# Routing weights of a fused two-layer kernel: ScalarE spreads them, the split is made after the transpose, and the scale products use four row groups

## The chip, the cores and the metric

The kernel runs on one core of one Trainium2 chip. The metric is the device time of one execution in microseconds; the time before is the median of three runs.

## What is computed

Input x has 2048 tokens (32 batches of 64) of 1024 features, float32. Two layers follow each other, each adding its result to x. Only the first one is touched by the change. Its core, cut to what matters:

```
y          = agg_w[b] @ x[b] + agg_b[b]           # 64x64 mix per batch
logits     = y @ gate_w.T                         # 1024 -> 8 experts
routing    = softmax(logits)                      # per token, 8 weights
in_scale   = routing @ in_channel_scale           # 8 -> 1024
out_scale  = routing @ out_channel_scale          # 8 -> 1024
x1         = x + (y * in_scale) @ sign(W).T * out_scale + bias
```

The second layer is a grouped convolution along the features, followed by a 1024x1024 product and a low-rank term with eight experts.

## The kernel before

The tokens are cut into 16 tiles of 128, taken in pairs (i, p). The program has a stage for each layer; the first runs over all tiles and writes x1 to a scratch tensor in DRAM, the second reads it back. Every engine has its own program, written out by hand in a fixed order with semaphores between them; loops run over the pairs, and nothing is reordered by a planner.

In the first stage TensorE works on two tiles at once. The large product of tile t (ffn0_step, L429) has 32 steps of 128x512: two output halves of 16, each half with the rounded part of the input (a = 0) and the rest (a = 1), so that float32 precision is kept with the faster float32r type. Between these steps stand the small products of tile t+1: ahead of step 0 the mixing product y (product_y, L382), ahead of step 12 (LOGITS_AT) the logits (product_logits, L391), ahead of step 20 (TURN_AT) the transpose of the routing weights (turn_routing, L397), ahead of step 24 (SCALES_AT) the products that make the two scales (product_in_scale, L405, and product_out_scale, L411).

Between the logits and the transpose stands a chain over two engines. VectorE takes the maximum (L756), ScalarE the exponentials and their sum (L601), VectorE the reciprocal (L758), the normalised weights (L762), a float32r copy of them (L766) and the rest that the rounding left (L768). The copies lie in the tile routing as 64 used columns: for the input scale two times [hi, hi, lo, lo] of 8 experts, for the output scale the same; 64 more columns are zero. After the transpose ScalarE copies 64 rows to routing_t (L605). The scales' weights scale_w hold hi and lo rows in the alternating order, so that one product over 32 rows gives all four terms of hi/lo. The input scale uses rows 0 to 31 for eight products of 128x128, the output scale rows 32 to 63 for two of 128x512. VectorE then multiplies y by the input scale (scale_in, L775), ScalarE rounds the product (round_parts, L610), and VectorE takes the rest (take_rest, L782). For the tile before, VectorE multiplies with the output scale (scale_out, L790), which ScalarE has copied out of PSUM (L621).

GpSimd does three kinds of SBUF work beside this: x plus bias (add_bias0, L895), the sum x1 (make_x1, L903), and the rests of the second layer's weights (rest_of_stage, L907), one chunk for every pair. SyncE issues the DMAs.

The first tile is special: nothing overlaps it, so y of both first tiles is made before the logits of the first (L435 to L438). The y of the second goes to banks 6 and 7, which the output scale would use, and the output scale of the first tile is therefore made later (L461 to L464), once VectorE has read these banks.

## Time and profile before

| | us |
|---|---|
| runs | 618.63, 617.22, 616.88 |
| median | 617.22 |
| profiled execution, first to last instruction | 617.4 |
| TensorE busy in it | 591.4 (96%) |
| VectorE busy | 252.3 (41%) |
| ScalarE busy | 113.5 (18%) |
| GpSimd busy | 147.0 (24%) |

The first stage lasts to about 249 us, the second takes the rest. TensorE's row says how long matmuls were under way, not that the array ran at its peak: matmuls are pipelined and weight loads are recorded apart (PEld). The chain of work that ended last is 89% TensorE, 4% VectorE and 1% ScalarE; the VectorE part is nearly all at the lines of the routing weights.

### The profile page before, as it was taken

Reading aid. Unit: us, or ns where it says so; the run is one execution under the profiler, and the core shown is the slowest. Engines: PE = TensorE matmul, PEld = TensorE weight load, DVE = VectorE, ACT = ScalarE, POOL = GpSimd, SP = SyncE. Lnnn points to the kernel's source line nnn. Section 1 sums busy time; section 2 is a strip of 40 time slices with the busy share of each in tenths; the row PEclk is TensorE's granted clock in tenths of the full one; section 3 lists DMA queues with packets and bytes.
Section 4 is the critical chain, followed back from the end, with each engine's and each line's share of the span. In section 5 each row is a group of like instructions: output and inputs, shape, how many; then the busy total and the mean of one; then the engine's idle time right before and its main releaser. Section 6 shows DMA issues by size and latency. Waiting matters only on the chain.

```text
span 617.4 us, 9165 instructions
## 1 busy us (share of the span) xinstructions
PE 591.4 (96%) x3381; PEld 516.5 (84%) x3381; DVE 252.3 (41%) x479; ACT 113.5 (18%) x255; POOL 147.0 (24%) x79
## 2 busy tenths in 40 slices
PE   4799999999999999999999999999999999999997
PEld 3677878778787878988988988988988998998996
DVE  4547766666775655623123123123123123123122
ACT  4522222222222213301101101101101101101100
POOL 0324345453444344801101101101101101101100
PEclk9769999999997999999999999999999999999999
DMA  9903242332323348512311312311321321321100
GB/s 291 355 1 112 89 140 102 108 110 72 110 84 98 112 131 188 141 63 45 107 70 37 106 71 35 106 72 34 106 74 32 106 75 31 106 78 28 69 35 34
DMA packets 36110, 58.15 MB, mean 94 GB/s; under 512 B 4096, under 2 KB 24384, under 8 KB 36096
## 3 DMA queue, kind: packets, MB, share of 16 engines
q1 hardware_dynamic: 35952, 57.70, 30.0%
q10 hardware_dynamic: 144, 0.26, 0.1%
q8 instruction: 10, 0.16, 0.1%
q14 instruction: 4, 0.03, 0.0%
HBM read 41.15 MB, written 16.79 MB: 94 GB/s over the span
## 4 chain that ended last, share of the span: by engine, by line
PE 89%; DVE 4%; ACT 1%; issue 0%; DVEq 0%
PE bank L498 47%; PE bank L429 17%; PE bank L480 9%; PE bank L391 4%; PE bank L382 4%; PE bank L526 4%; DVE gate L762 3%; PE bank L405 2%; PE bank L411 1%; PE bank L397 1%; ACT gate L601 1%; DVE routing L768 0%; DVE routing L766 0%; DVE gate L756 0%; DVE gate L758 0%
## 5 line engine op out<-in xcount | busy, mean ns | idle before, releaser
L498 PE MATMUL bank<-early,parts 128*128 128x320 f32 (+1 forms) x1152 | 206.5, 337 | 0.0
L498 PEld LDWEIGHTS bank<-early,parts 128*128 128x128 f32 x1152 | 184.7, 188 | 15.7
L429 PE MATMUL bank<-late,parts 128*128 128x512 f32 x512 | 140.6, 420 | 0.7 <-ACT parts L610 0.7
L429 PEld LDWEIGHTS bank<-late,parts 128*128 128x128 f32 x512 | 97.3, 200 | 22.9 <-issue 4.2
L935 POOL TENSOR_TENSOR work<-work,bias_bc 128x1024 f32<-128x1024 f32 x16 | 38.7, 2422 | 285.8 <-DMA work<-x_scratch 285.8
L498 PE MATMUL bank<-late,parts 128*128 128x512 f32 x384 | 93.9, 393 | 0.0
L498 PEld LDWEIGHTS bank<-late,parts 128*128 128x128 f32 x384 | 70.9, 188 | 15.8
L903 POOL TENSOR_TENSOR work<-work 128x512 f32<-128x512 f32 x32 | 40.8, 1276 | 80.4 <-DVE work L790 80.4
L480 PE MATMUL bank<-band,raw 128*128 128x128 f32 x512 | 59.7, 275 | 0.0
L480 PEld LDWEIGHTS bank<-band,raw 128*128 128x128 f32 x512 | 59.0, 192 | 0.1
L610 ACT ACTIVATE parts<-work 128x512 fp32r<-128x512 f32 x64 | 40.0, 633 | 74.8 <-DVE work L827 43.7
L782 DVE TENSOR_TENSOR parts<-work,parts 128x512 fp32r<-128x512 f32 x64 | 45.9, 739 | 12.0 <-ACT parts L610 10.5
L895 POOL TENSOR_TENSOR work<-xs,bias_bc 128x1024 f32<-128x1024 f32 x16 | 38.5, 2406 | 47.1 <-ACT late L594 24.6
L849 DVE TENSOR_TENSOR qk<-bank,qk 128x256 f32<-128x256 f32 x16 | 6.8, 424 | 100.5 <-ACT qk L666 100.5
L868 DVE TENSOR_TENSOR wh_t<-bank,wh_t 128x128 fp32r<-128x128 f32 x16 | 4.7, 292 | 95.0 <-ACT wh_t L674 95.0
L878 DVE TENSOR_TENSOR work<-bank,work 128x512 f32<-128x512 f32 x32 | 22.1, 692 | 50.4 <-PE bank L526 50.4
L382 PEld LDWEIGHTS bank<-agg,xs 128*128 128x128 f32 x256 | 34.6, 212 | 1.4 <-issue 0.2
L382 PE MATMUL bank<-agg,xs 128*128 128x128 f32 x256 | 34.8, 296 | 0.0
L391 PEld LDWEIGHTS bank<-cst,work 128*128 128x128 f32 x256 | 32.7, 200 | 1.3
L391 PE MATMUL bank<-cst,work 128*128 128x8 f32 x256 | 31.1, 257 | 0.0
L775 DVE TENSOR_TENSOR work<-bank,work 128x512 f32<-128x512 f32 x32 | 20.8, 687 | 23.7 <-PE bank L405 23.6
L526 PE MATMUL bank<-lora,wh_t 128*128 128x512 f32 x96 | 27.6, 396 | 0.0
(90 smaller groups left out, 363.5 us busy)
## 6 DMA issues: line engine op xcount, KB each, us to landing
xs<-in_x SPq DMA_DIRECT2D x16, 512.0 KB, 3.7
x_scratch<-work SPq DMA_DIRECT2D x16, 512.0 KB, 2.9
raw<-x_scratch SPq DMA_DIRECT2D x128, 64.0 KB, 3.1
work<-x_scratch SPq DMA_DIRECT2D x16, 512.0 KB, 3.6
out_tokens<-work SPq DMA_DIRECT2D x15, 512.0 KB, 2.7
stage<-in_wearly SPq DMA_DIRECT2D x8, 576.0 KB, 3.8
row_bc<-token_rows_scratch SPq DMA_DIRECT2D x30, 64.0 KB, 3.6
work<-in_wsign SPq DMA_DIRECT2D x3, 512.0 KB, 12.6
```

The costliest lines, as they stand in the source:

```text
L382: last = mm(bank[b0 + h][:, c * P:(c + 1) * P], xs[:, p, at:at + P], agg[:, p, :], start=True, stop=True)
L391: last = mm(bank[2][:, 0:E], y_t[:, c, :], cst[:, C_GATE + c * E:C_GATE + (c + 1) * E], start=(c == 0), stop=(c == L8 - 1))
L429: last = mm(bank[4 + h][:, :], parts[:, p, a, c, :], signs[:, c, h * HALF:(h + 1) * HALF], start=(k % 16 == 0), stop=(k % 16 == 15))
L480: last = mm(bank[n // 4][:, (n % 4) * P:(n % 4 + 1) * P], raw[:, p, n, s:s + P], band[:, s * GROUPS + n % 4, :], start=(s == 0), stop=(s = ...
L498: return mm(dst, parts[:, p, a, c, :], w(b, c), start=(k == 0), stop=(close and k == 23))
L526: last = mm(o[h][:, :], wh_t[:, a, :], lora[:, b, h * HALF:(h + 1) * HALF], start=False, stop=(k == 2))
L610: do(cols(parts[:, p, 0], h), cols(y_t, h), ACT.Copy).then_inc(done, 1)
L782: v.tensor_tensor(cols(parts[:, p, 1], h), cols(y_t, h), cols(parts[:, p, 0], h).bitcast(F32), ALU.subtract).then_inc(done, 1)
L878: v.tensor_tensor(o, bank[4 + 2 * p + h][:, :], o, ALU.add).then_inc(out_ready, 1)
L895: g.tensor_tensor(resid[:, p, :], xs[:, p, :], bias_bc[:, :], ALU.add).then_inc(xb_ready, 2)
L903: g.tensor_tensor(resid[:, p, cols], os_sb[:, cols], resid[:, p, cols], ALU.add).then_inc(x1_ready, 1)
L935: g.tensor_tensor(resid[:, p, :], resid[:, p, :], bias_bc[:, :], ALU.add).then_inc(resid_ready, 1)
```

## The change

The normalised weights are no longer made by VectorE. After the reciprocal, ScalarE multiplies the eight exponentials by it and writes them sixteen times side by side, as 128 plain float32 columns (spread_routing). After the transpose all 128 rows are in PSUM. ScalarE rounds them into routing_hi (round_routing), and VectorE makes routing_t in one instruction, (row factor times routing_hi) plus the PSUM rows (split_routing). The factor, a column of the constants, is 0 for the rows that should stay and minus 1 for those that should hold the rest.

The rows of scale_w now are four groups of 32: input scale left half, input scale right half, output scale left half, output scale right half. It is 128x512 instead of 64x1024. product_scales does the ten products in an order that goes round the groups. SCALES_AT goes from 24 to 26. On VectorE split_routing stands ahead of scale_out of the tile before. In the first tile, y of the second tile comes after the logits of the first and goes to banks 0 and 1, and the output scale is made with the input scale, so the separate later step is gone.

```diff
-LOGITS_AT, TURN_AT, SCALES_AT, CONV0_AT = 12, 20, 24, 8
+LOGITS_AT, TURN_AT, SCALES_AT, CONV0_AT = 12, 20, 26, 8
...
-            sp.dma_start(bias_bc[0:64, :], scales).then_inc(scales_loaded, 16)
+            sp.dma_start(bias_bc[:, 0:HALF], scales).then_inc(scales_loaded, 16)
...
-            def product_in_scale(i, p):
-                pe.wait_ge(routing_copied, 2 * i + p + 1)
-                for h in range(2):
-                    for c in range(4):
-                        at = (4 * h + c) * P
-                        last = mm(bank[2 + h][:, c * P:(c + 1) * P], scale_w[0:32, at:at + P], routing_t[0:32, :],
-                                  start=True, stop=True)
-                    last.then_inc(in_scale_done, 1)
-
-            def product_out_scale():
-                for h in range(2):
-                    mm(bank[6 + h][:, :], routing_t[32:64, :], scale_w[32:64, h * HALF:(h + 1) * HALF],
-                       start=True, stop=True).then_inc(out_scale_done, 1)
+            def product_scales(i, p):
+
+                pe.wait_ge(routing_split, 2 * i + p + 1)
+                for c in range(4):
+                    for h in range(2):
+                        rows = slice(32 * h, 32 * h + 32)
+                        made = mm(bank[2 + h][:, c * P:(c + 1) * P], scale_w[rows, c * P:(c + 1) * P],
+                                  routing_t[rows, :], start=True, stop=True)
+                        if c == 3:
+                            made.then_inc(in_scale_done, 1)
+                    if c < 2:
+                        rows = slice(64 + 32 * c, 96 + 32 * c)
+                        mm(bank[6 + c][:, :], routing_t[rows, :], scale_w[rows, :], start=True,
+                           stop=True).then_inc(out_scale_done, 1)
...
             product_y(0, 0)
-
-            product_y(0, 1, 6)
             product_logits(0, 0)
+            product_y(0, 1)
             pe.wait_ge(scale_ready, 1)
-            pe.wait_ge(routing_zeroed, 1)
             turn_routing(0, 0)
-            product_in_scale(0, 0)
+            product_scales(0, 0)
...
-                    if k == LOGITS_AT - 4 and first_tile:
-
-                        pe.wait_ge(y_biased, 4)
-                        product_out_scale()
...
-            def copy_routing(i, p):
+            def spread_routing(i, p):
+
+                act.wait_ge(gate_rcp, 2 * i + p + 1)
+                do(routing[:, :].rearrange("p (a e) -> p a e", e=E),
+                   gate[:, 8:16].rearrange("p (a e) -> p a e", a=1).broadcast_to([P, P // E, E]), ACT.Copy,
+                   scale=gate[:, 4:5]).then_inc(routing_ready, 1)
+
+            def round_routing(i, p):
                 act.wait_ge(routing_turned, 2 * i + p + 1)
-                do(routing_t[:, :], bank[3][0:64, 0:P], ACT.Copy).then_inc(routing_copied, 1)
+                do(routing_hi[:, :], bank[3][:, 0:P], ACT.Copy).then_inc(routing_rounded, 1)
...
                 v.reciprocal(gate[:, 4:5], gate[:, 1:2]).then_inc(gate_rcp, 1)
-                dve.wait_ge(gate_rcp, t1)
-
-                dve.wait_ge(routing_ready, t1 - 1)
-                v.tensor_scalar(gate[:, 32:40], gate[:, 8:16], gate[:, 4:5], None, ALU.mult).then_inc(gate_prob, 1)
-                dve.wait_ge(gate_prob, t1)
-
-                prob = gate[:, 32:40].rearrange("p (a b e) -> p a b e", a=1, b=1).broadcast_to([P, 2, 2, E])
-                v.tensor_copy(routing[:, 0:2, 0:2, :], prob).then_inc(routing_hi, 1)
-                dve.wait_ge(routing_hi, t1)
-                v.tensor_tensor(routing[:, 0:2, 2:4, :], prob, routing[:, 0:2, 0:2, :].bitcast(F32),
-                                ALU.subtract).then_inc(routing_ready, 1)
+
+            def split_routing(i, p):
+
+                dve.wait_ge(routing_rounded, 2 * i + p + 1)
+                v.scalar_tensor_tensor(routing_t[:, :], routing_hi[:, :].bitcast(F32), cst[:, C_RLO:C_RLO + 1],
+                                       bank[3][:, 0:P], ALU.mult, ALU.add).then_inc(routing_split, 1)
```

VectorE, one period of the first stage, before: L756 to L768 make the routing weights of the next tile, L790 is scale_out of this one, L775 and L782 are scale_in and take_rest.

```order
L756 TENSOR_REDUCE gate<-bank 128x1
L758 RECIPROCAL gate<-gate 128x1
L762 TENSOR_SCALAR gate<-gate 128x8
L766 CAST routing<-gate 128x2x16
L768 TENSOR_TENSOR routing<-gate,routing 128x2x16
L790 TENSOR_TENSOR work<-bank,work 128x512
L775 TENSOR_TENSOR work<-bank,work 128x512 x2
L782 TENSOR_TENSOR parts<-work,parts 128x512 x2
L790 TENSOR_TENSOR work<-bank,work 128x512
```

The same period after the change (the line numbers are those of the changed kernel: L755 is the maximum, L784 scale_out).

```order
L755 TENSOR_REDUCE gate<-bank 128x1
L757 RECIPROCAL gate<-gate 128x1
L762 SCALAR_TENSOR_TENSOR routing_t<-routing_hi,cst,bank 128x128
L784 TENSOR_TENSOR work<-bank,work 128x512
L769 TENSOR_TENSOR work<-bank,work 128x512 x2
L776 TENSOR_TENSOR parts<-work,parts 128x512 x2
L784 TENSOR_TENSOR work<-bank,work 128x512
```

Three small instructions before the transpose are gone, and one that waits for the transpose stands ahead of scale_out.

TensorE, one period, from the transpose (L397) to the end of the 32 steps (L429); L405 makes the input scale and L411 the output scale.

```order
 L397 MATMUL bank<-cst,routing 128x128
-L429 MATMUL bank<-late,parts 128x512 x4
-L405 MATMUL bank<-routing_t,scale_w 128x128 x8
-L411 MATMUL bank<-scale_w,routing_t 128x512 x2
-L429 MATMUL bank<-late,parts 128x512 x8
+L429 MATMUL bank<-late,parts 128x512 x6
+L405 MATMUL bank<-routing_t,scale_w 128x128 x2
+L411 MATMUL bank<-scale_w,routing_t 128x512
+L405 MATMUL bank<-routing_t,scale_w 128x128 x2
+L411 MATMUL bank<-scale_w,routing_t 128x512
+L405 MATMUL bank<-routing_t,scale_w 128x128 x4
+L429 MATMUL bank<-late,parts 128x512 x6
```

The ten products are the same in number and size; they stand two steps later and in mixed order.

TensorE in the first tile, up to the place where the scale products begin (L382 is y, L391 the logits).

```order
-L382 MATMUL bank<-agg,xs 128x128 x16
+L382 MATMUL bank<-agg,xs 128x128 x8
 L391 MATMUL bank<-cst,work 128x8 x8
+L382 MATMUL bank<-agg,xs 128x128 x8
 L397 MATMUL bank<-cst,routing 128x128
-L405 MATMUL bank<-routing_t,scale_w 128x128 x8
-L429 MATMUL bank<-late,parts 128x512 x8
-L411 MATMUL bank<-scale_w,routing_t 128x512 x2
-L429 MATMUL bank<-late,parts 128x512 x4
```

Eight products of y have moved behind the logits, and the output scale no longer stands between step 7 and step 8.

## Rows read from the trace of the kernel before

**Rows 1.** The page: the span, and TensorE's granted clock in forty slices

```profile
span 617.4 us, 9165 instructions
...
PEclk9769999999997999999999999999999999999999
```

**Rows 2.** Waits, all: engine, line, waited for, us in total, times, longest

```profile
PE bank L397 <- DVE routing L768: 11.3, 8, 1.6
```

**Rows 3.** Timeline, tile with a wait: start us, us, engine, line, operation [idle before]

```profile
106.35 0.17 DVE L756 TENSOR_REDUCE gate<-bank 128x1 f32<-128x8 f32 x1 [1.70 <-PE bank L391]
...
106.74 2.38 POOL L895 TENSOR_TENSOR work<-xs,bias_bc 128x1024 f32<-128x1024 f32 x1
...
107.14 2.00 DVE L762 TENSOR_SCALAR gate<-gate 128x8 f32<-128x8 f32 x1
...
109.64 0.33 PE L397 MATMUL bank<-cst,routing 128*128 128x128 f32 x1 [1.36 <-DVE routing L768]
```

**Rows 4.** Timeline, the tile before that one, which has no wait

```profile
92.76 2.37 POOL L895 TENSOR_TENSOR work<-xs,bias_bc 128x1024 f32<-128x1024 f32 x1 [3.17 <-DMA x_scratch<-work]
...
94.63 0.53 DVE L762 TENSOR_SCALAR gate<-gate 128x8 f32<-128x8 f32 x1
```

**Rows 5.** Two lines of stage two: duration ns min/median/max, first and last start

```profile
L862 DVE SCALAR_TENSOR_TENSOR wh<-gate,bank x16: 348/348/349, 259.5 to 604.1; 128x128 f32<-128x128 f32 x16
...
L674 ACT ACTIVATE wh_t<-bank x16: 277/278/279, 265.0 to 607.4; 128x128 fp32r<-128x128 f32 x16
```

**Rows 6.** Chain in order of time, around the scale products: start us, us, what

```profile
96.91 0.70 PE bank L405 x5
...
98.08 2.04 PE bank L429 x8
```

**Rows 7.** Timeline of weight loads and one matmul in the same scale products

```profile
96.84 0.63 PEld L405 LDWEIGHTS bank<-routing_t,scale_w 32*128 32x128 f32 x5 [0.36 <-issue]
...
97.35 0.18 PEld L411 LDWEIGHTS bank<-scale_w,routing_t 32*128 32x128 f32 x1
97.35 0.49 PE L411 MATMUL bank<-scale_w,routing_t 32*128 32x512 f32 x1
...
97.51 0.30 PEld L405 LDWEIGHTS bank<-routing_t,scale_w 32*128 32x128 f32 x2
```

**Rows 8.** The input scale's products: duration ns min/median/max

```profile
L405 PE MATMUL bank<-routing_t,scale_w x128: 267/271/468, 24.0 to 235.5; 32*128 32x128 f32 x128
```

**Rows 9.** Stretches: busy us of PE, PEld, DVE, ACT, POOL, then granted clock

```profile
137.00:143.00 6.00, 6.00 (x29) 4.62 (x28) 3.27 (x5) 1.71 (x3) 1.19 (x1) 0.72 0.00 0
193.00:201.00 8.00, 8.00 (x34) 6.81 (x34) 4.46 (x7) 2.35 (x4) 1.36 (x2) 0.57 0.02 8
```

**Rows 10.** Timeline of TensorE in the first tile

```profile
13.39 6.46 PE L382 MATMUL bank<-agg,xs 128*128 128x128 f32 x32
...
23.18 0.45 PE L397 MATMUL bank<-cst,routing 128*128 128x128 f32 x1 [1.65 <-DVE routing L768]
...
26.61 3.78 PE L429 MATMUL bank<-late,parts 128*128 128x512 f32 x8 [0.65 <-ACT parts L610]
32.16 1.22 PE L411 MATMUL bank<-scale_w,routing_t 32*128 32x512 f32 x2 [1.77 <-DVE work L749]
...
35.18 3.42 PE L391 MATMUL bank<-cst,work 128*128 128x8 f32 x16
...
42.00 0.41 PE L397 MATMUL bank<-cst,routing 128*128 128x128 f32 x1
```

**Rows 11.** Timeline of GpSimd and VectorE in the first tile

```profile
25.02 5.15 POOL L895 TENSOR_TENSOR work<-xs,bias_bc 128x1024 f32<-128x1024 f32 x2 [24.57 <-ACT late L594]
25.14 0.69 DVE L775 TENSOR_TENSOR work<-bank,work 128x512 f32<-128x512 f32 x1 [2.10 <-PE bank L405]
...
26.60 4.12 DVE L782 TENSOR_TENSOR parts<-work,parts 128x512 fp32r<-128x512 f32 x2
```

**Rows 12.** Stretch at the half clock in the first tiles, columns as in rows 9

```profile
33.30:42.10 8.80, 8.80 (x31) 7.53 (x30) 2.42 (x8) 2.07 (x5) 3.14 (x2) 0.50 0.01 2
```

More of the change, by code:

```diff
@@ L87, in adaln_ffn_kernel @@
         stage = sb("stage", [P, 2, NW])
-        scale_w = sb("scale_w", [64, H], F32R)
+        scale_w = sb("scale_w", [P, HALF], F32R)
         parts = sb("parts", [P, 2, 2, L8, P], F32R)
@@ L98, in adaln_ffn_kernel @@
         row_bc = sb("row_bc", [P, 2, P])
-        routing = sb("routing", [P, 4, 4, E], F32R)
-        routing_t = sb("routing_t", [64, P], F32R)
+        routing = sb("routing", [P, P])
+        routing_hi = sb("routing_hi", [P, P], F32R)
+        routing_t = sb("routing_t", [P, P], F32R)
         gate = sb("gate", [P, 64])
@@ L381, in product_y @@
                         at = (4 * h + c) * P
-                        last = mm(bank[b0 + h][:, c * P:(c + 1) * P], xs[:, p, at:at + P],
+                        last = mm(bank[h][:, c * P:(c + 1) * P], xs[:, p, at:at + P],
                                   agg[:, p, :], start=True, stop=True)
@@ L396, in turn_routing @@
                 pe.wait_ge(routing_ready, 2 * i + p + 1)
[L397 to L412 removed]
+                nc.tensor.transpose(bank[3][:, 0:P], routing[:, :], ident).then_inc(routing_turned, 1)
+            def product_scales(i, p):
[11 more added lines that the diff above has]
+                           stop=True).then_inc(out_scale_done, 1)
             def ffn0_step(i, p, k, first_tile=False):
@@ L585, in _ @@
             do(row_bc[:, :, :].rearrange("p a n -> p (a n)"), bank[4][:, 0:2 * P], ACT.Copy).then_inc(first_rows_ready, 1)
-            act.wait_ge(rows_loaded, 16)
             act.wait_ge(scales_loaded, 16)
-            do(scale_w[:, :], bias_bc[0:64, :], ACT.Copy, scale=rws[:, R_SG:R_SG + 1]).then_inc(scale_hi, 1)
+            do(scale_w[:, :], bias_bc[:, 0:HALF], ACT.Copy, scale=cst[:, C_SSG:C_SSG + 1]).then_inc(scale_hi, 1)
             def take_signs(c):
@@ L693, in _ @@
             v.memset(agg[:, :, :], 0.0).then_inc(agg_zeroed, 1)
-            v.memset(routing[:, 2:4, :, :].bitcast(F32), 0.0).then_inc(routing_zeroed, 1)
             dve.wait_ge(rows_loaded, 16)
@@ L795, in period0 @@
             def period0(i, p, ni, q, mix_next=True, first=False):
-                add_mix_bias(ni, q, b0=6 if first else 0, first_rows=first)
+                add_mix_bias(ni, q, first_rows=first)
                 if mix_next:
@@ L800, in period0 @@
                 route(ni, q)
+                split_routing(ni, q)
                 scale_out(i, p, 0)
@@ L807, in _ @@
             route(0, 0)
+            split_routing(0, 0)
             scale_in(0, 0)
@@ L970, in lay_out @@
     rows[0:K8, R_BK:R_BK + S] = f["L0_cond_bias_k"]
-    is_lo = (np.arange(64) // E) % 2
-    rows[:, R_LO] = is_lo
-    rows[:, R_SG] = 1 - 2 * is_lo
+    consts[:, C_RLO] = -((np.arange(P) // (2 * E)) % 2)
+    consts[:, C_SLO] = (np.arange(P) // E) % 2
+    consts[:, C_SSG] = 1 - 2 * consts[:, C_SLO]
     batch = np.arange(B)[:, None]
@@ L978, in lay_out @@
     mix = np.tile(f["L0_cond_weight"].reshape(K8, S, S).transpose(2, 1, 0), (2, 1, 1))
-    scales = np.concatenate([np.tile(perm(f["L0_ffn_in_channel_scale"], 1), (4, 1)),
-                             np.tile(perm(f["L0_ffn_out_channel_scale"], 1), (4, 1))])
+    scales = np.concatenate([np.tile(perm(f[name], 1)[:, h * HALF:(h + 1) * HALF], (4, 1))
+                             for name in ("L0_ffn_in_channel_scale", "L0_ffn_out_channel_scale") for h in range(2)])
     wsign = turned(perm(f["L0_ffn_weight"], 0))
```

29 lines of the change are left out of this document (13 added, 16 removed).

## The prediction

> **What bounds the kernel now.** First the page: the profiled execution spans 617.4 us and the median of the runs is 617.22 us, so what lies around the span is nothing that counts (0.2 us less), and the sum below is made against 617.4. TensorE is busy 96% of the span, and its granted clock is full in nearly all of the forty slices, with dips at the start and twice in the first third [rows 1]. So only what TensorE does or waits for counts, and since the change touches the first stage only, the second (from 249 us on) keeps its length.
>
> Then the waits. One is repeated: the transpose of the routing weights (L397) waits for VectorE's last routing instruction, 8 times, 11.3 us in total [rows 2]. The first of them, in the first tile, is 1.65 us [rows 10], so seven in the steady part hold 9.7 us, 1.38 us each.
>
> Then the timeline of one such tile. After the logits, VectorE's maximum starts at 106.35. The normalising instruction L762, on eight columns, takes 2.00 us and ends at 109.14, and GpSimd's L895, from 106.74 for 2.38 us, ends at 109.12 [rows 3]. In the tile before, which has no wait, L762 takes 0.53 us and ends at 95.16, with GpSimd's L895 ending at 95.13 [rows 4]. So the small instruction ends when GpSimd's ends, whatever its own work: it is held by the SBUF work of GpSimd. In every second tile GpSimd is later, because the weight rests (L907) stand in front of L895, and there TensorE has to wait.
>
> **The wait before the transpose.** The change takes L762, L766 and L768 off the path and puts one ScalarE instruction there. Price of the spread, 128 columns: the trace has no such form from SBUF; the nearest row is a 128x128 copy out of PSUM, 0.278 us [rows 5]. I take 0.32, with 0.28 and 0.45 as ends. From the maximum's start to the end of the reciprocal 0.76 us pass (106.35 to just before 107.14 [rows 3]), with 0.05 for the semaphore and 0.32 the weights are ready 1.15 us after it, at 107.5. TensorE came free at 109.64 - 1.36 = 108.28. The wait is gone with 0.8 us in hand, even at the dear end. Term: **-9.7 us**.
>
> Would GpSimd hold something else instead? The new VectorE instruction L762 (split) reads one tensor in SBUF and one in PSUM. A VectorE instruction with the same kinds of operands, L775, started at 25.14 inside GpSimd's 25.02 to 30.17 and took its usual 0.69 us, while L782, with both tensors in SBUF, needed 4.12 us for two [rows 11]. So the split should not be held.
>
> **The wait before the scale products.** The split costs more after the transpose than the old copy did. Transpose 0.33 [rows 3], rounding on ScalarE 0.28, split 0.35 [rows 5], three semaphores of 0.04: 1.08 us. TensorE has six steps there instead of four; eight steps take 2.04 us [rows 6], so six take 1.53. The cover is 0.45 us; if it fails, TensorE pays the difference in each of 15 tiles. Queued behind the split on VectorE is scale_out of the tile before, which began before the transpose and now ends some 1.8 us after it. GpSimd's x1 waits for it, and so does step 0 of the next tile, which comes after the scale products, six steps and y, over 3 us later; scale_in, next on VectorE, has its data no earlier than that. I cost it at nothing. The six steps and y that follow the scale products (1.5 + 1.8 us) must hide scale_in, the rounding and the first rest: 0.69 + 0.63 + 0.69 = 2.0 us. They do.
>
> **The scale products.** Now the ten take 98.08 - 96.91 = 1.17 us [rows 6]. The five weight loads of one row group begin in 0.63 - 0.19 = 0.44 us, 0.11 us apart, and L411, in the other row group, starts in between without moving them: L405's last two still start from 97.51, and L411 itself is 0.49 us under way [rows 7]. So products of different row groups run side by side and those of one group follow at 0.11 us. After the change the longest group has four products instead of eight: 4 x 0.11 = 0.44 us less. The two 512-column products begin third and sixth and are within that time nearly. I take 0.40 us less for each of 15 tiles: **-6.0 us**. Bounds: 0.5 us less each (-7.5), and ten loads in a row at 0.11, that is two steps more than the eight of now, +0.22 (+3.3).
>
> The Trainium skill, TensorEngine Tiling, section Theoretical Speedup, promises up to four times for contractions of 32 rows or less. By that the block would shrink from 1.17 to 0.29 us and the term would be -13 us. The rows above show one overlap of two groups and not four, so the page's figure carries no part of the sum. The same page, section Key Properties, says that changing the tiling mode drains TensorE, which speaks against more switching; between the groups of one size the rows show no drain.
>
> **The clock.** In two stretches, 137 to 143 and 193 to 201 us, the mean granted clock is 0.72 and 0.57 [rows 9]: 3.4 and 6.9 us at the lower level, 1.2 GHz, which cost half of that, 5.1 us. Both follow a tile in which TensorE had been idle before the transpose; in the whole second stage, without such waits, the clock never falls [rows 1]. I expect them gone: **-5.1 us**, with 0 as the other end.
>
> **The first tile.** Two waits stand there: 1.65 us before the transpose, and 1.77 us before the output scale at 32.16 [rows 10]. The first is filled by the second y (half of 6.46 us [rows 10]), which stood ahead of the logits. As the chain from logits to step 0 grows by the split and by a y that has to be finished, step 0 begins only some 0.4 us before 26.61. The second wait goes with the output scale: it waited for VectorE's rests, held by GpSimd (4.12 us for two [rows 11]), and for the bias after them. Now steps 8 to 11 go on at once (four at 0.43 = 1.7 us, where 35.18 - 32.16 = 3.0 us passed) and the logits wait for the bias, which comes at 32.1 - 0.4 - 0.7 = 31.0. The second logits start near 31.4 instead of 35.18: 3.8 us. All this ran at the lower clock, still 0.50 from 33.3 to 42.1 [rows 12]. If the clock rises as long after work becomes continuous as it did there, it does so near 35 instead of 42, ahead of the transpose at 42.00 - 3.8 = 38.2; the 3.2 us between are then done in half. Together 5.4; I take **-5.0 us**, with -3 and -8 as ends. The smaller edits (a shorter scale_w, its load over 128 rows, no zeroing of routing) lie beside TensorE's work.
>
> **Sum.** 617.4 - 9.7 - 6.0 - 5.1 - 5.0 = 591.6 us of span, less 0.2: 591.5.
>
> **Rivals.**
> - The scale products get no cheaper: four groups share something that two did not. The term is then 0 to +3.3 instead of -6: 597.5 to 601. For it: only two groups are seen together. Against it: nothing in the step of 0.11 us moved when the second group came in.
> - The clock still falls twice in the first stage: 596.6. For it: the ten small products use a part of the array only. Against it: no fall without a wait in the second stage.
> - The split is held by GpSimd after all. In every second tile L895 runs over the time of the split, 0.9 us more than the cover: seven times 0.9 is 6.3, so 598. Against it stands L775 [rows 11].
> - Slower than before: each switch of row group waits for the matmul before it. The products would then stand one behind the other at their full durations, eight at 0.27 [rows 8] and two at 0.49 [rows 7], 3.1 us instead of 1.17, in 16 tiles +32 us: 591.5 + 6 + 32 = 629.5. It decides from about 2.4 us for the block, where the other terms are used up (19.8 us over 16 tiles is 1.2 us). Now there is one switch, then nine. Against it: the first switches in the rows cost nothing.
> - The change does not do what it says: the weights come as late as before, because ScalarE is not free when the reciprocal ends: about 617. Against it: its two instructions end before 107 and it waits for the transpose.
>
> **How the numbers follow.** Chances: the forecast 0.63, no cheaper products 0.15, clock 0.12, held split 0.05, switches 0.03, no effect 0.02. The range from 586.5 to 602.0 holds the forecast with its own ends (first tile at -8, products at -7.5) and the first three rivals with little more than 0.05 outside them; the rest of the 0.2 is for two rivals at once. About 0.3% is what a measurement of this kernel can tell from no change. Faster by more than that: 0.95; the same: 0.02; slower: 0.03.
>
> **What would show it.** In the changed kernel the waits list should have no entry of the transpose for a routing instruction beyond the first tile; the transpose should follow the eighth step at once; the distance from the first scale product to the next step should be near 0.8 us; L762 (split) should take 0.35 us in all tiles, also under GpSimd's L895; the tile period should be near 12.3 us throughout; the granted clock should stay at 1.00 from about 35 us on. The forecast is wrong if a wait of the scale products for the split appears, if their block stays at 1.1 us or more, or if the clock's dips remain.

## The result and the profile after

| | before | after |
|---|---|---|
| runs, us | 618.63, 617.22, 616.88, 617.7 | 585.94, 587.87, 587.86, 585.37 |
| median, us | 617.46 | 586.9 |
| ratio (95% interval) | | 0.950 (0.948 to 0.952) |
| span of the profiled execution, us | 617.4 | 584.2 |
| mean granted clock in it | 0.974 | 0.994 |

The forecast was 591.5 with a range from 586.5 to 602.0. Executions of the kernel after fall into two groups 2 us apart (585.4 to 585.9 and 587.9) and those of before spread over some 3 us (616.9 to 618.6 here), the profiled execution of before is one of the longer and that of after one of the shorter, and spans are compared below within a group as far as their times tell it.

The page of the kernel after, which answers [rows 1]: the span, busy time of the engines, and the granted clock in forty slices.

```profile
span 584.2 us, 9131 instructions
...
PE 569.8 (98%) x3381; PEld 502.3 (86%) x3381; DVE 232.6 (40%) x446; ACT 118.9 (20%) x271; POOL 148.1 (25%) x79
...
PEclk9889999999999999999999999999999999999999
```

The dips of the slices in the middle of the first stage are gone. So is the repeated wait of [rows 2]: this is TensorE's part of the list of waits from the first y on (line, waited for, us, times, longest), and no entry has L397 in it.

```profile
PE bank L429 <- ACT parts L609: 1.5, 1, 1.5
PE bank L405 <- DVE routing_t L762: 1.0, 1, 1.0
...
PE bank L391 <- DVE work L748: 0.5, 1, 0.5
```

Each of the three stands once, before the second transpose. Behind that TensorE waits for nothing that the profile shows in the first stage.

The timeline of a tile in which GpSimd's sum (now L891) runs, to set beside [rows 3, 4]. Columns: start us, us, engine, line, operation, idle before and its releaser. L598 is the spread, L604 the rounding, L762 now the split.

```profile
80.13 0.17 DVE L755 TENSOR_REDUCE gate<-bank 128x1 f32<-128x8 f32 x1 [1.16 <-PE bank L391]
80.19 2.41 POOL L891 TENSOR_TENSOR work<-xs,bias_bc 128x1024 f32<-128x1024 f32 x1 [3.20 <-DMA x_scratch<-work]
...
80.92 0.40 ACT L598 ACTIVATE routing<-gate 128x128 f32<-128x128 f32 x1 [0.23 <-DVE gate L757]
...
81.90 0.27 PE L397 MATMUL bank<-cst,routing 128*128 128x128 f32 x1
...
82.52 0.35 DVE L762 SCALAR_TENSOR_TENSOR routing_t<-routing_hi,cst,bank 128x128 fp32r<-128x128 f32 x1 [1.64 <-ACT routing_hi L604]
...
83.49 0.33 PE L405 MATMUL bank<-routing_t,scale_w 32*128 32x128 f32 x2
```

The weights are ready at 81.32, 1.19 us after the maximum began, while GpSimd works until 82.60. TensorE takes them at 81.90, behind its eighth step. The split ends at 82.87, the first scale product starts 0.62 us later.

The two new instructions over all 16 tiles (duration in ns: least, median, most; first and last start), to set beside [rows 5]; the single product of L405 is unchanged, 267 to 325 ns against [rows 8]:

```profile
L598 ACT ACTIVATE routing<-gate x16: 400/402/403, 20.0 to 199.4; 128x128 f32<-128x128 f32 x16
...
L762 DVE SCALAR_TENSOR_TENSOR routing_t<-routing_hi,cst,bank x16: 346/347/348, 21.5 to 201.0; 128x128 fp32r<-128x128 f32 x16
```

The chain of work that ended last, in order of time (start us, us, what), in the same tile, for [rows 6]:

```profile
82.06 0.11 PE bank L397
82.17 1.39 PE bank L429 x6
83.56 0.26 PE bank L405 x2
83.81 0.10 PE bank L411
83.92 0.23 PE bank L405 x5
84.15 1.58 PE bank L429 x6
...
93.90 0.11 PE bank L397
```

The ten scale products hold the chain from 83.56 to 84.15, 0.59 us where it was 1.17. The tile's period is 93.90 - 82.06 = 11.84 us, for 12.3 forecast. A second thing is in the chain and was in no term of the forecast: the transpose's piece is 0.11 us. In the kernel before it was three times as long in 13 of the 14 tiles from the third transpose on (0.31 or 0.33 us), also in six of the seven without a listed wait. Its chain in the tile of [rows 6], with the second transpose and the start of the second stage (L498):

```profile
42.21 0.21 PE bank L397
...
95.67 0.31 PE bank L397
...
248.73 1.31 PE bank L498 x9
```

The same two places in the kernel after (L491 is now the second stage):

```profile
34.52 0.21 PE bank L397
...
215.16 1.90 PE bank L491 x13
```

From the second transpose to the second stage 206.52 us have become 180.64; the second stage, from there to the end of the span, took 368.7 and takes 369.0.

TensorE in the first tile, for [rows 10]:

```profile
21.94 0.33 PE L405 MATMUL bank<-routing_t,scale_w 32*128 32x128 f32 x2 [0.97 <-DVE routing_t L762]
...
24.11 4.62 PE L429 MATMUL bank<-late,parts 128*128 128x512 f32 x12 [1.50 <-ACT parts L609]
29.22 1.92 PE L391 MATMUL bank<-cst,work 128*128 128x8 f32 x16 [0.50 <-DVE work L748]
```

The waits before the transpose (1.65) and before the output scale (1.77) of [rows 10] have gone. In their place stand 0.97 for the split and 0.50 for the bias, and the wait before step 0 has grown from 0.65 to 1.50. VectorE's two rests are still held by GpSimd there, as in [rows 11]:

```profile
24.09 4.21 DVE L776 TENSOR_TENSOR parts<-work,parts 128x512 fp32r<-128x512 f32 x2 [0.16 <-ACT parts L609]
```

The first stretch of [rows 9] in the kernel after, same columns (the second has a clock of 1.00 too; busy us of PE, PEld, DVE, ACT, POOL, then granted clock):

```profile
137.00:143.00 6.00, 6.00 (x42) 4.96 (x40) 2.44 (x6) 2.00 (x5) 4.83 (x2) 1.00 0.72 214
```

### The profile page after: what moved, and what is told of

The parts are those of the page before. It is cut to its first block, busy times and chain, and to the rows that moved or that the text cites. A ratio compares the mean times of both kernels' runs of the same rounds, so it can differ in the third digit from the quotient of the medians.

```text
span 584.2 us, 9131 instructions
## 1 busy us (share of the span) xinstructions
PE 569.8 (98%) x3381; PEld 502.3 (86%) x3381; DVE 232.6 (40%) x446; ACT 118.9 (20%) x271; POOL 148.1 (25%) x79
## 4 chain that ended last, share of the span: by engine, by line
PE 94%; DVE 0%; issue 0%
PE bank L491 49%; PE bank L429 21%; PE bank L473 10%; PE bank L391 4%; PE bank L382 4%; PE bank L519 4%; PE bank L405 1%; PE bank L397 0%; PE bank L512 0%; PE bank L411 0%; DVE work L748 0%; DVE work L874 0%
## 5 line engine op out<-in xcount | busy, mean ns | idle before, releaser
L491 PE MATMUL bank<-early,parts 128*128 128x320 f32 (+1 forms) x1152 | 206.5, 337 | 0.0
L491 PEld LDWEIGHTS bank<-early,parts 128*128 128x128 f32 x1152 | 184.7, 188 | 15.7
L429 PE MATMUL bank<-late,parts 128*128 128x512 f32 x512 | 134.5, 411 | 1.5 <-ACT parts L609 1.5
L429 PEld LDWEIGHTS bank<-late,parts 128*128 128x128 f32 x512 | 93.5, 193 | 21.9 <-ACT parts L609 1.9
L491 PE MATMUL bank<-late,parts 128*128 128x512 f32 x384 | 94.2, 394 | 0.0
L491 PEld LDWEIGHTS bank<-late,parts 128*128 128x128 f32 x384 | 70.9, 188 | 16.1
L891 POOL TENSOR_TENSOR work<-xs,bias_bc 128x1024 f32<-128x1024 f32 x16 | 38.7, 2424 | 45.3 <-DMA x_scratch<-work 23.1
L874 DVE TENSOR_TENSOR work<-bank,work 128x512 f32<-128x512 f32 x32 | 22.1, 692 | 50.7 <-PE bank L519 50.7
L382 PEld LDWEIGHTS bank<-agg,xs 128*128 128x128 f32 x256 | 32.5, 200 | 1.4 <-issue 0.2
L391 PEld LDWEIGHTS bank<-cst,work 128*128 128x128 f32 x256 | 31.4, 194 | 2.0 <-issue 0.9
L382 PE MATMUL bank<-agg,xs 128*128 128x128 f32 x256 | 33.0, 285 | 0.0
L391 PE MATMUL bank<-cst,work 128*128 128x8 f32 x256 | 30.1, 253 | 0.5 <-DVE work L748 0.5
L664 ACT ACTIVATE qk<-bank 128x64 f32<-128x64 f32 x16 | 3.6, 225 | 119.0 <-PE bank L491 119.0
```

Of the source, the lines that this page charges most:

```text
L382: last = mm(bank[h][:, c * P:(c + 1) * P], xs[:, p, at:at + P], agg[:, p, :], start=True, stop=True)
L391: last = mm(bank[2][:, 0:E], y_t[:, c, :], cst[:, C_GATE + c * E:C_GATE + (c + 1) * E], start=(c == 0), stop=(c == L8 - 1))
L429: last = mm(bank[4 + h][:, :], parts[:, p, a, c, :], signs[:, c, h * HALF:(h + 1) * HALF], start=(k % 16 == 0), stop=(k % 16 == 15))
L491: return mm(dst, parts[:, p, a, c, :], w(b, c), start=(k == 0), stop=(close and k == 23))
L874: v.tensor_tensor(o, bank[4 + 2 * p + h][:, :], o, ALU.add).then_inc(out_ready, 1)
L891: g.tensor_tensor(resid[:, p, :], xs[:, p, :], bias_bc[:, :], ALU.add).then_inc(xb_ready, 2)
```

## The experiments

Twelve kernels were run, in three batches (e1 to e4, e5 to e8, e9 to e12), each on another chip. Each batch had its own runs of the kernel before, to which the ratios refer; their medians were 617.47, 616.09 and 617.37 us. The kernel after was not run in them, so against it a difference of less than about 1.5 us can't be told from medians alone. Diffs are against the kernel after, unless said.

**One row group or two instead of four.** Does the gain of the products come from the row groups, or from the mixed order?

e1_two_groups:

```diff
-                        rows = slice(32 * h, 32 * h + 32)
+                        rows = slice(0, 32)
...
-                        rows = slice(64 + 32 * c, 96 + 32 * c)
+                        rows = slice(64, 96)
```

> The changed kernel with the ten scale products in two row groups instead of four: both halves of the input scale from rows 0 to 31, both of the output scale from rows 64 to 95, in the same order. It leaves out that the halves have weights of their own, so its output is not that of the layer; the work is the same in number and size. If products of different row groups run side by side and those of one group follow at 0.11 us, the longest group has eight again: the block goes from 0.59 to 1.0 to 1.17 us, the kernel from 586.9 to 594 to 596. If instead the gain came from the order of the products or from the copies out of PSUM, it stays at 587.

e2_one_group has `slice(0, 32)` in both places.

> The changed kernel with all ten scale products in one row group, rows 0 to 31, in the same order; as in e1 the output scale and the right half of the input scale get the wrong weights. By the theory of side-by-side groups nothing overlaps: eight products at 0.11 and two at 0.22 us, with the start 1.5 to 1.6 us for the block instead of 0.59, times 16: 601 to 603. If the block is bound by issue, it stays under 1 us and the kernel under 593.

Measured: e1 592.1 us, ratio 0.964 (0.956 to 0.971), with one execution of 600.47 among three at 591.9 to 592.3, of which there is no trace and for which nothing was found. e2 601.89 us, ratio 0.974 (0.971 to 0.977). The block of e1 in its chain:

```profile
84.94 0.25 PE bank L405
...
85.53 0.45 PE bank L405 x4
85.98 1.58 PE bank L429 x6
```

and of e2:

```profile
89.83 0.36 PE bank L405 x2
...
91.33 1.59 PE bank L429 x6
```

The end of the block in the kernel before, in the tile of [rows 6]:

```profile
97.61 0.11 PE bank L411
97.73 0.22 PE bank L405 x2
97.95 0.13 PE bank L411
```

The block lasts 1.50 us in one group, 1.04 in two and 0.59 in four. The kernel before, with two groups and the two output products among the last, had 1.17: the order, with another pair of rows in e1, is worth 0.13, the step from two groups to four 0.45. In the span e1 is 590.4 and the kernel after 584.2 (same group), 6.2 us, where 15 times 0.45 is 6.75. e2 is 600.4 against 586.0 in the longer group, 14.4, where 15 times 0.91 is 13.7. e1 came 2 us below what was expected (594 to 596), e2 as expected. The rivals "no cheaper" and "switches cost" fall.

The four groups gain 2.5 times over one. The Trainium skill, TensorEngine Tiling (Array Packing), section Theoretical Speedup, gives up to four times for contractions of 32 rows. An estimate from that figure is 1.50 / 4 = 0.38 us for the block; the measurement, 0.59, decides.

**The order of the first tile.** e3_old_first_tile puts the old order back: the second y ahead of the logits and into banks 6 and 7, the output scale apart.

```diff
             product_y(0, 0)
+            product_y(0, 1, 6)
             product_logits(0, 0)
-            product_y(0, 1)
...
-            product_scales(0, 0)
+            product_scales(0, 0, False)
...
+                    if k == LOGITS_AT - 4 and first_tile:
+                        pe.wait_ge(y_biased, 4)
+                        product_out(0)
+                        product_out(1)
```

> The changed kernel with the first tile's order of before: the second tile's y ahead of the first logits and in banks 6 and 7, the output scale of the first tile ahead of step 8. The second transpose began at 42.0 us before and at 34.3 us after. If the new order brought most of these 7.7 us, it begins near 40 and the kernel takes 592 to 593; if they came from the four row groups, the split and the clock alone, it begins by 36 and the kernel takes under 589.

Measured: 592.96 us, ratio 0.960 (0.958 to 0.963), as expected. Its timeline has the wait for the output scale back, and the second transpose comes when it came in [rows 10]:

```profile
32.09 0.79 PE L401 MATMUL bank<-scale_w,routing_t 32*128 32x512 f32 x2 [1.37 <-DVE work L755]
...
41.52 0.41 PE L397 MATMUL bank<-cst,routing 128*128 128x128 f32 x1
```

The order of the first tile is worth 6 us, and it is separable from the rest. A part of it is TensorE's rate: the second logits take 3.42 us in e3 and 1.92 in the kernel after. Behind that tile e3 has the same periods as the kernel after, with the granted clock at 1.00 from 42 to 220 us.

**Only the hold.** e4_before_psum is the kernel before with one thing changed: the exponentials and their normalised form lie in PSUM.

```diff
-                do(gate[:, 8:16], bank[2][:, 0:E], ACT.Exp, bias=gate[:, 0:1], accum_out=gate[:, 1:2]).then_inc(gate_exp, 1)
+                do(bank[2][:, 16:24], bank[2][:, 0:E], ACT.Exp, bias=gate[:, 0:1], accum_out=gate[:, 1:2]).then_inc(gate_exp, 1)
...
-                v.tensor_scalar(gate[:, 32:40], gate[:, 8:16], gate[:, 4:5], None, ALU.mult).then_inc(gate_prob, 1)
+                v.tensor_scalar(bank[2][:, 32:40], bank[2][:, 16:24], gate[:, 4:5], None, ALU.mult).then_inc(gate_prob, 1)
...
-                prob = gate[:, 32:40].rearrange("p (a b e) -> p a b e", a=1, b=1).broadcast_to([P, 2, 2, E])
+                prob = bank[2][:, 32:40].rearrange("p (a b e) -> p a b e", a=1, b=1).broadcast_to([P, 2, 2, E])
```

> The kernel before, with one edit: ScalarE writes the exponentials to PSUM, and VectorE's three routing instructions read (and the first also writes) there, so that none of them has two operands in SBUF or the two-port form; number, engine and order are those of before. Theory of the hold by GpSimd: L762 takes about 0.2 us in all tiles, whether GpSimd runs or not, the waits before the transpose go, the clock stays up after the first tiles: 617.5 - 9.7 - 5.1, perhaps 2.8 more: 600 to 603. Rival, that the chain over VectorE is too long by itself: 614 to 617.

Measured: 600.46 us, ratio 0.974 (0.971 to 0.976), as expected. The normalising instruction over all tiles, then in one tile beside GpSimd's sum:

```profile
L762 DVE TENSOR_SCALAR bank<-bank,gate x16: 232/234/235, 21.4 to 213.8; 128x8 f32<-128x8 f32 x16
```

```profile
87.87 2.38 POOL L895 TENSOR_TENSOR work<-xs,bias_bc 128x1024 f32<-128x1024 f32 x1 [3.16 <-DMA x_scratch<-work]
...
89.76 0.23 DVE L762 TENSOR_SCALAR bank<-bank,gate 128x8 f32<-128x8 f32 x1
```

It took up to 2.06 us before and takes 0.23 in every tile, with GpSimd at work around it. The transpose's piece of the chain is 0.11 us in all tiles behind the second transpose, and the dips of the clock are gone (granted clock 1.00 from 44 to 240 us). Two operands moved to PSUM give 17.0 of the 30.6 us, without ScalarE's spread and without more row groups. The Trainium skill, SBUF — State Buffer, section Who interferes with whom, says that a VectorE instruction with at most one SBUF input, outside its two-port modes, does not contend with GpSimd, and that a tensor_scalar in such a mode is blocked whole by whoever has the ports. The traces agree with the first in times, 0.234 us here and 0.347 for the split with one input in each memory, against up to 2.06 for the form in SBUF alone; whether that form ran in a two-port mode they don't tell.

**Only the normalising back on VectorE.** e5_vector_normalises is the kernel after, with the eight-column product on VectorE, in SBUF, and ScalarE only spreading.

```diff
-                   gate[:, 8:16].rearrange("p (a e) -> p a e", a=1).broadcast_to([P, P // E, E]), ACT.Copy,
-                   scale=gate[:, 4:5]).then_inc(routing_ready, 1)
+                   gate[:, 32:40].rearrange("p (a e) -> p a e", a=1).broadcast_to([P, P // E, E]),
+                   ACT.Copy).then_inc(routing_ready, 1)
...
+                v.tensor_scalar(gate[:, 32:40], gate[:, 8:16], gate[:, 4:5], None, ALU.mult).then_inc(gate_prob, 1)
```

> The changed kernel, but VectorE multiplies the eight exponentials by the reciprocal, in SBUF, as before the change, and ScalarE only spreads the result. One VectorE instruction of 0.23 us more in the chain. If only its length counted, nothing would move (0.5 us are in hand before the transpose): 587 to 588. By the theory of the hold it ends with GpSimd's instruction, which runs there in both kinds of tile now (80.2 to 82.6, and 90.8 to 93.4 followed by one to 95.8): waits of 1 us or more before the transpose in most of 14 tiles, 600 to 612, and the clock falls again in the first stage.

Measured: 596.77 us, ratio 0.968 (0.964 to 0.971). A tile of it:

```profile
81.88 2.38 POOL L894 TENSOR_TENSOR work<-xs,bias_bc 128x1024 f32<-128x1024 f32 x1 [3.20 <-DMA x_scratch<-work]
...
82.62 1.68 DVE L760 TENSOR_SCALAR gate<-gate 128x8 f32<-128x8 f32 x1
...
84.69 0.33 PE L398 MATMUL bank<-cst,routing 128*128 128x128 f32 x1 [0.94 <-ACT routing L599]
```

The hold is back: the small product ends at 84.30, GpSimd at 84.26. The mechanism is the expected one, but the forecast of 600 to 612 was missed, since the price was set too high: of the 14 tiles behind the second transpose only every second one has a listed wait, 0.94 to 1.39 us and 7.3 in all, and no dip of the clock came with them. In the other seven the transpose comes late without a listed wait: its piece is 0.29 to 0.33 us. From the second transpose to the second stage e5 takes 190.9 us, 10.3 more than the kernel after. The listed 7.3 and some 0.2 us more at each of the 14 transposes (2.9 in all) make 10.2 of it.

**Was the step from 24 to 26 needed?** e6_scales_24:

```diff
-LOGITS_AT, TURN_AT, SCALES_AT, CONV0_AT = 12, 20, 26, 8
+LOGITS_AT, TURN_AT, SCALES_AT, CONV0_AT = 12, 20, 24, 8
```

> The changed kernel with the scale products ahead of step 24 again instead of 26. The split ends 0.62 us before the first scale product in the changed kernel, two steps are 0.46 us. If the move to 26 was needed, a wait of the scale products or of their weight loads comes up in 15 tiles: 589 to 592. If the cover of 0.45 us that the prediction took was too small, no difference: 586.5 to 588.

Measured: 587.88 us (585.28 to 588.19), ratio 0.952 (0.949 to 0.955): no difference that can be told. By its time its profiled execution is of the longer group, as is that of the kernel before, so it serves for the sum below: span 586.0, start of the second transpose and of the second stage at

```profile
36.33 0.34 PE bank L397
...
217.03 2.05 PE bank L491 x14
```

**A transpose without reserve.** e7_turn_18 has TURN_AT 18 instead of 20, so that the weights come just in time.

> The changed kernel with the transpose ahead of step 18 instead of 20. The weights are then ready about 0.1 us before TensorE comes there. In the trace of before a transpose whose weights were ready only just in time took 0.31 us of the chain, after the change it takes 0.11. If a load that can't be issued ahead costs these 0.2 us, the kernel gets 2.5 to 3.5 us slower although no wait of TensorE is long: 589.5 to 590.5. If not, 586.5 to 587.5.

Measured: 588.54 us (588.21 to 588.78), ratio 0.954 (0.951 to 0.957). That lies between the two forecasts and only 0.7 above e6, too little to tell. The trace decides: in the tile at 84 us the weights are ready at 83.80, the transpose's weight load starts at 83.85 and the transpose at 83.92 (the load ran 0.23 us ahead in the kernel after), and the transpose's piece of the chain is still 0.11 us. The extra 0.2 us of the kernel before is therefore not the price of a weight load that cannot run ahead; it comes only when the weights are later than TensorE.

**Waits put back.** Two kernels put waits of known length before the transpose, by copies on ScalarE ahead of the spread whose output nobody reads. e9_long_waits has three of 128x512 in every second tile, e10_short_waits two of 128x448 in every tile:

```diff
+                if p == 1:
+                    for m in range(3):
...
+                        do(qk[:, :, :].rearrange("p a n -> p (a n)")[:, 0:512].rearrange("p (a e) -> p a e", e=E),
+                           gate[:, 8:16].rearrange("p (a e) -> p a e", a=1).broadcast_to([P, 512 // E, E]), ACT.Copy,
+                           scale=gate[:, 4:5]).then_inc(hold_done, 1)
```

> The changed kernel with three dummy ScalarE instructions (128x512, 0.63 us each) ahead of the spread, in every second tile (8 of 16), writing to a tile that the first stage doesn't use. The transpose of these tiles then waits as long as in the kernel before, about 1.5 us. By length alone: 7 or 8 times 1.5 is 10.5 to 12 us: 597.5 to 599. If waits of this length bring the clock down as in the kernel before (granted clock 0.974 to 0.981 there, 0.983 to 0.986 in e3 with its first tile and without waits), the mean clock is 0.985 or less against 0.994 to 1.0 and the time 600 to 603.

> The same idle time cut in shorter waits: two dummy ScalarE instructions of 128x448 (0.58 us each) in all 16 tiles, about 0.7 us of wait each, 10.5 us in total: 597 to 598.5. If it is the length of a single wait that brings the clock down, its mean stays at 0.99 or more here. If it is the sum of the idle time, it falls as in e9. The wait that the trace shows will be some 0.17 us shorter than what the tile's period grows by, if a matmul's modelled end (0.39 us after its start, where the next can start after 0.23) hides the start of the idle time.

Measured: e9 599.62 us (599.45 to 602.4), ratio 0.973 (0.969 to 0.976), mean clock 0.994 in three executions and 0.988 in one. e10 602.55 us (601.28 to 604.79), ratio 0.976 (0.972 to 0.980), mean clock 0.991 to 1.0. The waits that their lists show, e9 and then e10:

```profile
PE bank L398 <- ACT routing L606: 11.9, 8, 1.5
```

```profile
PE bank L398 <- ACT routing L606: 10.5, 15, 1.2
```

and the transposes of two tiles in the chain of e9, the first with a wait, the second without:

```profile
87.01 0.33 PE bank L398
...
99.07 0.11 PE bank L398
```

Two things follow. First, a wait costs more than its entry. e9's span is 598.0 against 584.2, 13.8 us for 11.9 shown. Within one trace it is plainer: two tiles of e9 with one wait of 1.52 between their transposes take 87.01 - 61.58 = 25.43 us, two of the kernel after 23.69, so the wait costs 1.74; a tile of e10 takes 12.72 us instead of 11.84, 0.88 for a wait of 0.66. That is 0.22 us for each wait over its entry, and the chain shows where: 0.33 instead of 0.11 at the transpose. A matmul of a step is recorded for 0.41 us on average, while the next follows after 0.25 (eight in 1.97), so the first 0.16 us of idle time lie under the modelled end of the last one and stand in no wait; the rest is that the late transpose is recorded for 0.33 us instead of 0.27. e10 missed its forecast of 597 to 598.5. Its waits came as planned (10.5 us in all), but the forecast added the listed waits alone, and 15 times 0.22 is 3.3 more; the two executions without a loss of clock, 601.28 and 601.73 us, lie 13.6 above the longer group of the kernel after. The other two, 603.38 and 604.79, had a mean clock of 0.991 and 0.993; in the traced one of them (603.38) the loss lies before 45 us, not in the middle of the stage.

Second, eight waits of 1.5 us, as long and as often as those of [rows 2], did not bring the clock down in three of four executions; in the traced one it is 1.00 from 45 us to the end. Of the fourth there is no trace. The rival that the length of the waits alone made the dips of [rows 9] isn't supported.

**Can the first tile be shortened further?** Three kernels try. e8_gpsimd_later holds GpSimd's first sums back until VectorE's rests are done:

```diff
             pool.wait_ge(bias0_loaded, 16)
+            pool.wait_ge(u_lo, 2)
             add_bias0(0, 0, True)
```

> The changed kernel, with GpSimd's first two additions (x plus bias, 5.16 us) held back until VectorE has taken the two rests of the first tile, which took 4.21 us for two while GpSimd ran, 1.29 otherwise. The bias for the second logits then comes 2.9 us sooner, and steps 4 to 11 don't wait; TensorE's own steps now bound this stretch. Theory of the hold: 1.5 to 3 us faster, 584 to 585.5. If the rests were slow for another reason: 587.

e11_fill lets TensorE multiply constants into banks that are free (17 products of 128x128) where it waits in the first 25 us:

```diff
+            fill(7, 5)
             pe.wait_ge(att_tiled, 1)
...
+            fill(7, 2)
             pe.wait_ge(att_rep_ready, 1)
...
             turn_routing(0, 0)
+            fill(5, 4)
             product_scales(0, 0)
+            fill(5, 6)
```

> The changed kernel with 17 dummy matmuls (128x128, float32) where TensorE waits in the first 25 us: 7 in the chain of the small network at the start, 4 after the first transpose, 6 after the first scale products. The runs of the changed kernel fall in two groups, 585.4 to 585.9 and 587.9, as the clock comes up early or not. If the low clock of the first tiles is due to the idle time there, the filled kernel lies at 583 to 585 in all runs. If the fills only delay the chain, it is at 587 to 589.

e12_fill_and_hold is both.

> e11 and e8 together: the fills, and GpSimd's first two additions held back until the rests of the first tile are made. e8 alone brought nothing, since TensorE at the low clock needed 5.5 us for the twelve steps that the hold delays. With the clock up these steps take 2.8 us and the hold decides: then 1.5 to 2 us faster than e11, 581.5 to 583.5. If the clock stays low, the same as e11.

Measured: e8 587.81 us (587.66 to 588.39), ratio 0.953 (0.950 to 0.956), no gain where 584 to 585.5 was forecast. e11 588.75 us (588.0 to 593.22), ratio 0.955 (0.952 to 0.958), no gain. e12 583.4 us (583.14 to 586.95, seven executions), ratio 0.945 (0.942 to 0.947), within the forecast of 581.5 to 583.5, though 5.4 below e11 and not 1.5 to 2: faster than both kernels, by 3.5 us against the kernel after. TensorE after the first scale products in e8, e11 and e12 (the steps in e8 and e12, the logits that wait and the steps behind them in e11):

```profile
27.14 5.46 PE L429 MATMUL bank<-late,parts 128*128 128x512 f32 x12 [1.50 <-ACT parts L609]
```

```profile
30.13 2.64 PE L396 MATMUL bank<-cst,work 128*128 128x8 f32 x16 [1.55 <-DVE work L755]
32.62 3.76 PE L434 MATMUL bank<-late,parts 128*128 128x512 f32 x8
```

```profile
28.14 3.01 PE L434 MATMUL bank<-late,parts 128*128 128x512 f32 x12
```

In these traces either cause covers for the other. With GpSimd held back VectorE needs 1.29 us for the two rests instead of 4.21, but the twelve steps run at the half rate and take 5.46 us. With the fills alone TensorE has done the twelve steps by 28.6 and waits 1.55 us for VectorE, which GpSimd holds; behind that wait it is at the half rate again (granted clock 0.50 from 32 to 36 us), 3.76 us for eight steps where e12 takes 2.11. With both the twelve steps take 3.01 us and nothing waits before the logits. But the trace of e12 is of an execution of 586.91 us, one of the two longer among the seven. What the five of 583.1 to 583.5 do otherwise in their first tile no trace shows, so the gain is measured and its cause in part argued.

## Why the prediction came out as it did

The forecast was right in sign, 4.6 us too long, and the median lies within the range by 0.4 us, with some luck: two of the four executions (585.37 and 585.94) lie below its end of 586.5, and the range had no room for the term that was missed. The ends that it names, -8 for the first tile and -7.5 for the products, add up to 587.0. The terms, in the span, with e6's execution for the changed kernel (same group as the profiled execution of before, 617.4 against 586.0):

| term | forecast | measured |
|---|---|---|
| wait before the transpose | -9.7 | -9.7 (no entry left beyond the first tile) |
| scale products | -6.0 | 15 x (0.59 - 1.17) = -8.7 |
| weights 0.2 us late in 13 of 14 tiles | not seen | 12 x (0.11 - 0.33) + (0.11 - 0.31) = -2.8 |
| clock | -5.1 | -4.6, what is left of 206.5 - 180.7 |
| first tile, to the second transpose | -5.0 | 36.33 - 42.21 = -5.9 |
| second stage | 0 | 369.0 - 368.7 = +0.3 |
| sum | -25.8 | -31.4 |

The two executions are paired by their times alone, and ahead of the first transpose they are not alike: the first logits take 1.85 us in the kernel before and 3.42 in e6. So the term of the first tile is uncertain by some 2 us. From the kernel after's own trace it would be 34.52 - 42.21 = -7.7; the terms behind it stay as they are.

- **Wait before the transpose**: right. The spread cost 0.402 us, inside its ends of 0.28 and 0.45, and weights were ready 1.19 us after the maximum began, for 1.15 forecast. e4 and e5 show the cause from both sides: take the small product's SBUF operands away and the hold goes, bring them back and it is back.
- **Scale products**: right in mechanism, mis-sized, and even beyond its own bound of -7.5. The step that failed is the one from the number of products in the longest group: I took the eight of L405 against four, 0.11 us each. But in the block of before I put the two output products of the second group at nothing. They cost 0.11 and 0.13 us in its chain, and four groups hide these too: ten products at 0.06 each in the place of ten at 0.12.
- **Weights 0.2 us late**: a term that the working missed. It called a tile "without a wait" because the waits list had none. But in that tile L762 took 0.53 us beside GpSimd [rows 4] where it takes 0.23 when it isn't held, and the chain's 0.31 at the transpose, just ahead of [rows 6], should have been held against the 0.11 of the single output product L411 behind it. Both kinds of tile were held, one of them for less time. e4 takes the amount away and e5 brings it back.
- **Clock**: the size was nearly right, the dips are gone in the kernel after and in e3, e4 and e5. The cause is not shown. The prediction said that the waits bring the clock down; e9 put waits of that length back and had no dip in three of four executions. What else of the kernel before takes part stays open.
- **First tile**: nearly right in size, through partly wrong steps. Step 0 was forecast 0.4 us earlier and came 0.5 later (27.12 in e6 for 26.61; 24.11 in the shorter execution of the kernel after), because the waits for the split and for the parts (1.51) take what the transpose's wait gave. The second logits were forecast at 31.4 and came at 32.18. But the full rate came with them and not near 35, so that they took 1.84 us for the 3.42 of [rows 10]. That the gain belongs to this order is shown by e3.
- **Cover of the split**: 0.62 us for 0.45 forecast; e6 shows that even two steps less would have been enough.
- **Held split** (rival): the split takes 346 to 348 ns in all tiles, so it fell. **No cheaper products** and **switches**: fell by e1 and e2. The drain that the prediction cites belongs to a change of mode, and both kernels go from full rows to 32 rows and back once per tile, so it spoke neither for nor against the nine steps from group to group. **Clock still falls**: fell by the stretches above.
- **Span and time**: the working put 0.2 us off the span to reach the median. In every run that has both, the time is 1.7 to 1.9 us above the span (584.2 and 585.94). The profiled execution of before was simply one of the longer ones. Carried through, the forecast of the span would have meant 593.4 in its group.

## What to carry to other kernels

When a tiny VectorE instruction on the critical path ends just as GpSimd ends, move its operands to PSUM or the work to ScalarE before anything else: two operands gave 17 us here. Spreading small products with a contraction of 32 rows over row groups and going round the groups shortens their block (1.50, 1.04, 0.59 us for ten products in one, two, four groups). Look in the chain, not only in the waits list: a transpose whose piece is 0.3 us where its neighbours are 0.1 is waiting, though no wait is listed.

## What the runs showed of the hardware that was not expected

- Idle time of up to some 0.2 us before a matmul is not in the waits list, since it lies under the modelled end of the one before. A listed wait is short by about the same amount (0.22 us for each in e9 and e10).
- At the start the recorded clock does not fit the rate. In e6's profiled execution the stretch from 12 to 28 us is recorded at 1.00, while the sixteen matmuls of the logits take 3.42 us there, and 1.84 us at 32 us, in the same record. Whether the record lacks a stretch at the lower level or something else halved the rate is not shown:

```profile
16.50 3.42 PE L391 MATMUL bank<-cst,work 128*128 128x8 f32 x16
...
32.18 1.84 PE L391 MATMUL bank<-cst,work 128*128 128x8 f32 x16
```

- Moving VectorE's work in time moved a hold to another instruction: L719 (L720 in the kernel before), two inputs in SBUF, took 0.68 to 0.69 us before and takes 0.69 to 1.48 us after. In the later tiles it lies beside TensorE's work and costs nothing. In the first tile of e6 it is in the chain that ended last, from 32.22 for 1.42 us, and the second transpose, at 36.33, has a wait of 0.36 us at the end of the chain behind it.
- ScalarE's copy of 128 columns from SBUF with a scale operand took 0.402 us, without one 0.31 (e5), and the 128x128 copy out of PSUM 0.278 [rows 5].
